# A post-layernorm block of attention and mixture of experts, fp32: V and row-sum strips grouped over two steps, and the token list made by matmuls

## The reference

```python
def _L0_attn_ref(x, wq, bq, wk, bk, wv, bv, wo, bo):
    def proj(w, b):
        return (x @ w.T + b).reshape(B, S, HEADS, HEAD_DIM).transpose(0, 2, 1, 3)
    q = proj(wq, bq)
    k = proj(wk, bk)
    v = proj(wv, bv)
    scores = jnp.einsum('bhqd,bhkd->bhqk', q, k) / scale
    probs = jax.nn.softmax(scores, axis=-1)
    ctx = jnp.einsum('bhqk,bhkd->bhqd', probs, v)
    ctx = ctx.transpose(0, 2, 1, 3).reshape(B, S, HIDDEN)
    return ctx @ wo.T + bo
...
    # _L0_ffn_ref: 8 experts of 256, each token goes to its best 2, plus a shared expert of 512
    scores = xf @ gate_w.T
    ew, ei = jax.lax.top_k(scores, TOP_K)
    ew = jax.nn.softmax(ew, axis=-1)
    routed = jnp.einsum('te,ted->td', comb, expert_out)
    shared = jax.nn.silu(xf @ sh_gate.T) * (xf @ sh_up.T) @ sh_down.T
    sgate = jax.nn.sigmoid(xf @ se_gate_w.T)
    return (routed + sgate * shared).reshape(Bb, Tt, Cc)
x = _layernorm(x + _L0_attn_ref(x, ...), axis=-1)
x = _layernorm(x + _L0_ffn_ref(x, ...), axis=-1)
```

## Time and profile before

| | |
|---|---|
| median of 3 runs | 2303.1 us (2297.88 to 2305.36) |
| the profiled execution | 2299.8 us, its span 2298.1 us |
| PE busy | 2130.9 us (93%) |
| PEld, DVE, ACT, POOL busy | 1177.7, 1212.6, 851.8, 953.1 us |
| mean granted clock of PE | 0.972 |
| DMA | 202.83 MB, mean 88 GB/s |

### The profile page before, as it was taken

How to read it: one execution, slowest core, us unless ns; L and a number is a source line. 1 busy time by engine, 2 the same in 40 slices (tenths; PEclk the granted TensorE clock), 3 DMA queues, 4 the chain that set the end, 5 groups by cost and what they waited for, 6 DMA issues and landing times. The chain is left out here.

```text
span 2298.1 us, 34596 instructions
## 1 busy us (share of the span) xinstructions
PE 2130.9 (93%) x9524; PEld 1177.7 (51%) x9525; DVE 1212.6 (53%) x2169; ACT 851.8 (37%) x1508; POOL 953.1 (41%) x926
## 2 busy tenths in 40 slices
PE   7999999999999999999999986791899999999997
PEld 5544445445445445445555422470754444445886
DVE  6767665567665566665567723450222222223875
ACT  2355553355553355554355662320111111111332
POOL 1245753454753454754454564427021111112651
PEclk9999999999999999999999998895999999999999
DMA  4230333221433221333221303560132222223762
GB/s 137 65 71 29 94 70 89 80 61 30 100 68 93 80 48 42 98 70 76 95 55 26 75 11 111 197 256 0 53 105 90 91 90 84 90 91 116 228 184 77
DMA packets 96850, 202.83 MB, mean 88 GB/s; under 512 B 26912, under 2 KB 27424, under 8 KB 94752
## 3 DMA queue, kind: packets, MB, share of 16 engines
q1 hardware_dynamic: 83744, 165.04, 24.6%
q0 software_dynamic: 12928, 35.70, 5.7%
HBM read 110.68 MB, written 39.13 MB: 65 GB/s over the span
## 5 line engine op out<-in xcount | busy, mean ns | idle before, releaser
L765 DVE TENSOR_REDUCE max_half<-ps_side 128x1 f32<-128x512 f32 x1024 | 663.5, 683 | 335.4 <-PE ps_side L532 326.1
L683 ACT ACTIVATE probs<-ps_s 128x512 f32<-128x512 f32 x1024 | 573.4, 596 | 485.9 <-PE ps_s L549 391.2
L469 POOL TENSOR_TENSOR acc<-probs 128x512 f32<-128x512 f32 x384 | 484.7, 1289 | 486.5 <-ACT probs L683 480.8
L549 PE MATMUL ps_s<-kq_stack 97*128 97x512 f32 x1024 | 461.5, 454 | 23.5 <-ACT probs L683 14.4
L532 PE MATMUL ps_side<-kq_stack 96*128 96x512 f32 x1024 | 399.8, 401 | 10.9 <-DVE max_half L765 7.2
L549 PEld LDWEIGHTS ps_s<-kq_stack 97*128 97x128 f32 x1024 | 192.6, 189 | 361.0 <-ACT probs L683 222.3
L560 PE MATMUL ps_ctx<-probs,v_sb 128*32 128x512 f32 x2048 | 274.5, 608 | 0.0
L1433 PE MATMUL ps_gu<-gu_sb,xT_e 128*128 x576 | 261.3, 596 | 0.5 <-issue 0.3
L1331 POOL DMA_INDIRECT x_g<-x,who_all x72 | 67.8, 941 | 389.0 <-PE ps_t L1423 325.7
L532 PEld LDWEIGHTS ps_side<-kq_stack 96*128 96x128 f32 x1024 | 195.9, 191 | 44.9 <-DVE max_half L765 13.8
L1433 PEld LDWEIGHTS ps_gu<-gu_sb,xT_e 128*128 128x128 f32 x576 | 103.7, 190 | 107.7 <-issue 107.3
(11 more groups left out here) (194 smaller groups left out, 2477.5 us busy)
## 6 DMA issues: line engine op xcount, KB each, us to landing
kq_stack<-kq SPq DMA_DIRECT2D x192, 256.0 KB, 5.1
y_slots<-y_t SPq DMA_DIRECT2D x72, 256.0 KB, 2.3
res<-inv_rows SPq DMA_DIRECT2D x128, 64.0 KB, 2.0
probs<-x SPq DMA_DIRECT2D x16, 512.0 KB, 5.1
x_r<-x SPq DMA_DIRECT2D x32, 256.0 KB, 3.7
x_t<-x SPq DMA_DIRECT2D x32, 256.0 KB
gu_sb<-wgu SPq DMA_DIRECT2D x8, 1024.0 KB, 14.9
out<-gu_sb SPq DMA_DIRECT2D x32, 256.0 KB, 2.6
```

Source lines behind the costliest of these rows:

```text
L469: nc.gpsimd.tensor_tensor(acc[:, h, :], probs[:, (loc - 1) % 2, h, :] if j == 1 else acc[:, h, :], probs[:, loc % 2, h, :], ALU.add).then_ ...
L549: nc.tensor.matmul(ps_s[:, (loc * HG + h) % RING, :], k_stack[par][0:3 * HD + 1, h, kt * P:(kt + 1) * P], q_stack[par][0:3 * HD + 1, h, ha ...
L683: nc.scalar.activation(probs[:, loc % 2, h, :], ps_s[:, (loc * HG + h) % RING, :], ACT.Exp, scale=HD ** -0.5).then_inc(probs_ready, 1)
L765: nc.vector.reduce_max(max_half[:, u // 2, u % 2:u % 2 + 1], bank, AX.X).then_inc(side_free, 1)
```

## The change

1. `weighted` for two steps is called at the end of the odd step, followed by `row_sums`: one group of strips per two steps. So the probabilities need three buffers (`PROBS`). The middle one lies in the place of V's low weights `wv_lo`, which are saved to DRAM at the start and loaded back before each later making of V. The exponentials wait for the strips three steps before.
2. The projection pieces are at slots 0, 4, 8, ... 60 of the group, one per step.
3. The banks of V's and the output's tiles are turned by three, and waits at the batch's edge follow the new buffers.
4. The token list: for each slot of the list a matmul sums one-hot rows (place in the tile) times one-hot columns (tile) scaled with the token number, 64 matmuls of 128 x 128 x 72 into one bank, prepared by DVE in eight parts (two behind each of tiles 3 to 6), done by PE two parts behind each of tiles 4 to 7, copied by DVE after tile 7. The scatters, the table and its load are gone.

```diff
@@ -31,13 +31,14 @@
 SLOTS = 4
-PROJ_FROM, PROJ_EVERY, PROJ_UNIT = 2, 3, 14
+PROJ_FROM, PROJ_EVERY, PROJ_UNIT = 0, 4, 16
 LOW_LATER = 2
...
 FOLD = 2
+PROBS = 3
 FOLD_DVE = 1
@@ -87,6 +88,7 @@
+    wv_lo_kept = nc.dram_tensor("wv_lo_kept", (P, C, D), F32, kind="Internal").ap()
     inv_rows = nc.dram_tensor("inv_rows", (HG, HALF), F32, kind="Internal").ap()
@@ -107,6 +109,8 @@
         wv_hi = sb("wv_hi", [P, C, D], F32R)
+        with nc.sbuf_tensor("probs_mid", [P, HG, HALF], F32) as probs_mid:
+            pass
         wv_lo = sb("wv_lo", [P, C, D], F32R)
@@ -122,7 +126,12 @@
         v_sb = sb("v_sb", [P, KT, D])
-        probs = sb("probs", [P, 2, HG, HALF])
+        probs_outer = sb("probs_outer", [P, 2, HG, HALF])
+        def probs(loc, h):
+            return probs_mid[:, h, :] if loc % PROBS == 1 else probs_outer[:, loc % PROBS // 2, h, :]
         ctx_sb = sb("ctx_sb", [P, G, S])
...
@@ -199,9 +209,13 @@
+        def tail_bank(i):
+            return ps_side[:, (i + SIDE_RING) % TAIL_RING, :]
         def res_of(t):
-            return x_nat[:, t - 2, :] if 2 <= t < 6 else res[:, t % 2, :]
+            return probs_mid[:, t - 2, :] if 2 <= t < 6 else res[:, t % 2, :]
@@ -325,6 +339,11 @@
                                              for h in (1, 2)} if x_chunks else {})
+                if not last and g == G - 1:
+                    sp.wait_ge(pv_done, (b + 1) * BSTEPS - FOLD)
+                    sp.wait_ge(sum_done, (b + 1) * SUMS - 1)
+                    sp.sem_inc(passed_sp, 1)
+                    sp.dma_start(wv_lo[:].bitcast(F32), wv_lo_kept).then_inc(wv_moved, 16)
                 if not (last and g == G - 1):
@@ -367,6 +386,8 @@
             spread(0, 0)
+            sp.wait_ge(wv_split, C)
+            sp.dma_start(wv_lo_kept, wv_lo[:].bitcast(F32)).then_inc(wv_moved, 16)
             row(-1, -1, 0, False)
@@ -466,8 +487,8 @@
                         pool.wait_ge(folded, (b * FOLDS + folds(loc) - 2) * FOLD_POOL + h + 1)
-                    nc.gpsimd.tensor_tensor(acc[:, h, :], probs[:, (loc - 1) % 2, h, :] if j == 1 else acc[:, h, :],
-                                            probs[:, loc % 2, h, :], ALU.add).then_inc(folded, 1)
+                    nc.gpsimd.tensor_tensor(acc[:, h, :], probs(loc - 1, h) if j == 1 else acc[:, h, :],
+                                            probs(loc, h), ALU.add).then_inc(folded, 1)
@@ -559,7 +580,7 @@
                                             v_sb[:, kt, (g * HG + h) * HD:(g * HG + h + 1) * HD],
-                                            probs[:, loc % 2, h, :], start=kt == 0, stop=kt == KT - 1)
+                                            probs(loc, h), start=kt == 0, stop=kt == KT - 1)
                 done.then_inc(pv_done, 1)
@@ -599,13 +620,13 @@
                         if loc == 0 and slot < SIDE_RING:
-                            pe.wait_ge(tail_free, b * TAIL + KT - (2 - slot if slot < 2 else 0) - (slot < 2))
+                            pe.wait_ge(tail_free, b * TAIL + KT - (SIDE_RING - 1 - slot))
                         for kind, u, place in side_in(last, loc, slot):
                             side_unit(b, b * G + g, g, kind, u, place)
-                        if slot == SLOTS - 1:
-                            weighted(b, loc)
-                            if loc % FOLD == FOLD - 1:
-                                row_sums(b, loc)
+                        if slot == SLOTS - 1 and loc % FOLD == FOLD - 1:
+                            for done in range(loc - FOLD + 1, loc + 1):
+                                weighted(b, done)
+                            row_sums(b, loc)
@@ -628,13 +649,14 @@
                 pe.wait_ge(side_free, base_of(b * G + G))
+                pe.wait_ge(wv_moved, 16 * (b + 2))
                 for t in range(KT):
-                    v_tile(b * TAIL + KT + t, t, ps_side[:, t % TAIL_RING, :], TAIL_RING)
+                    v_tile(b * TAIL + KT + t, t, tail_bank(t), TAIL_RING)
                 pe.wait_ge(wo_in, 16 * (b + 1))
...
                         pe.wait_ge(ctx_done, (b + 1) * G * NHALF - (t == 0))
-                    o_tile(b * TAIL + 2 * KT + t, t, ps_side[:, (KT + t) % TAIL_RING, :],
+                    o_tile(b * TAIL + 2 * KT + t, t, tail_bank(KT + t),
                            [wo[:, g, :] for g in range(G)])
...
@@ -669,18 +691,18 @@
                 act.wait_ge(scores_ready, b * HEADS_B + HG * loc + h + 1)
-                if loc >= 2:
-                    act.wait_ge(pv_done, b * BSTEPS + loc - 1)
-                    if h < FOLD_POOL:
-                        act.wait_ge(folded, (b * FOLDS + folds(loc - 2) - 1) * FOLD_POOL + h + 1)
-                    else:
-                        act.wait_ge(folded_dve, (b * FOLDS + folds(loc - 2) - 1) * FOLD_DVE + h - FOLD_POOL + 1)
-                else:
-                    if h == 0:
-                        act.wait_ge(tail_free, b * TAIL + KT // 2 * (loc + 1))
-                    if loc == 0:
-                        act.wait_ge(x2_out[h + 2], 16 * (b + 1))
-                nc.scalar.activation(probs[:, loc % 2, h, :], ps_s[:, (loc * HG + h) % RING, :],
+                if loc >= PROBS:
+                    act.wait_ge(pv_done, b * BSTEPS + loc - PROBS + 1)
+                    act.wait_ge(sum_done, b * SUMS + (loc - PROBS) // FOLD + 1)
+                elif loc == 0:
+                    act.wait_ge(tail_free, b * TAIL + (KT if isinstance(b, int) and b == 0 else h + 1))
+                elif loc == 1:
+                    if isinstance(b, int) and b == 0:
+                        act.wait_ge(wv_moved, 16)
+                    act.wait_ge(x2_out[h + 2], 16 * (b + 1))
+                elif h == 0:
+                    act.wait_ge(tail_free, b * TAIL + KT)
+                nc.scalar.activation(probs(loc, h), ps_s[:, (loc * HG + h) % RING, :],
                                      ACT.Exp, scale=HD ** -0.5).then_inc(probs_ready, 1)
...
@@ -1079,6 +1101,14 @@
+TABLE_PARTS = 8
+PART = 2 * TT // TABLE_PARTS
+COUNT_COLUMNS_AFTER = 3
+TABLE_AFTER = {3: (0, 1), 4: (2, 3), 5: (4, 5), 6: (6, 7)}
+LOOK_UP_AFTER = {4: (0, 1), 5: (2, 3), 6: (4, 5), 7: (6, 7)}
+WHO_AFTER = 7
 def combine_plan():
...
@@ -1255,17 +1289,12 @@
                 load_tile(t)
-            sp.wait_ge(made, 5)
-            sp.dma_start(table.rearrange("(p n) a -> p (n a)", p=P), zero_table[:]).then_inc(zeroed, 16)
             for e in range(E):
...
                 load_tile(t + 4)
-                if t == COVER - 3:
-                    sp.wait_ge(scattered, 16 * 2 * TT)
-                    sp.dma_start(who_all[:], table.rearrange("(p n) a -> p (n a)", p=P)).then_inc(who_in, 16)
@@ -1308,21 +1337,10 @@
             after(nc.gpsimd.memset(all_ones[:], 1.0))
-            after(nc.gpsimd.memset(zero_table[:], 0))
             after(nc.gpsimd.affine_select(out=tri[:], in_=all_ones[:], compare_op=ALU.is_gt, fill=0.0, base=0,
...
             after(nc.gpsimd.memset(minus_half[:], -0.5))
-            pool.wait_ge(placed, 1)
-            pool.wait_ge(zeroed, 16)
-            pool.sem_inc(passed, 1)
-            for t in range(TT):
-                for v in range(2):
-                    nc.gpsimd.indirect_dma_start(
-                        table, bass.IndirectOffsetOnAxis(ap=col_i[4][:, v, t:t + 1].bitcast(U32), axis=0),
-                        token[:, t:t + 1], None).then_inc(scattered, 16)
-            pool.wait_ge(who_in, 16)
+            pool.wait_ge(who_known, 1)
             pool.sem_inc(passed, 1)
@@ -1458,6 +1476,14 @@
+            def look_up(part):
+                pe.wait_ge(part_made, part + 1)
+                for c in range(PART):
+                    done = nc.tensor.matmul(ps_who, in_tile[:, part % 2, c, :], of_tile[:, part % 2, c, :],
+                                            start=part == 0 and c == 0, stop=part == TABLE_PARTS - 1 and c == PART - 1)
+                done.then_inc(part_read, 1)
             def expert_of(t):
@@ -1482,11 +1508,16 @@
                 if t == 1:
-                    pe.wait_ge(made, 6)
+                    pe.wait_ge(made, 5)
                     pe.wait_ge(visits, 1)
...
                     nc.tensor.matmul(ps_total, all_ones[:], flat, start=True, stop=True).then_inc(counted, 1)
+                if t == COUNT_COLUMNS_AFTER:
+                    pe.wait_ge(ranked, 1)
+                    nc.tensor.matmul(ps_count, all_ones[:], tri[:], start=True, stop=True).then_inc(columns_made, 1)
+                for part in LOOK_UP_AFTER.get(t, ()):
+                    look_up(part)
@@ -1725,7 +1756,8 @@
                 link(v.tensor_tensor(big[3], src[:], first[:], ALU.subtract))
-                link(v.tensor_tensor(big[3], big[3], ps_rank.rearrange("p (t e) -> p t e", e=E), ALU.add))
+                v.tensor_tensor(big[3], big[3], ps_rank.rearrange("p (t e) -> p t e", e=E), ALU.add).then_inc(ranked, 1)
+                dve.wait_ge(ranked, 1)
                 return src
@@ -1758,15 +1790,35 @@
                 link(v.tensor_copy(rows[:, 1], col_i[1][:]))
```

(27 more changed lines are left out.)

36 lines of the change are left out of this document (20 added, 16 removed).

## The result

The kernel after takes 2375.05 us (2373.86 to 2376.1 in four runs), the kernel before 2303.39 beside it: a ratio of 1.0315 [1.0297, 1.0333]. The change makes the kernel slower, close to the forecast of 2374. The profiled execution took 2376.1 us, its span 2374.4.

The account below looks back on a forecast made before the run. PE's own instruction stream bounds the kernel, with a stall in the shared expert's tiles and attention partly paced by the score ring. Terms -51 - 39 + 58 + 5 + 4 + 55 + 42 = +74 on 2299.8: 2374 us, range 2308 to 2418.

Parts of the forecast that it names:

- The list: MoE token list by matmuls: 65 us of stall removed, 14 us of PE passes added, DVE's work hidden; net -51 us.
- A pass: One of 128 fp32 lookup passes on PE: 0.11 us each, 14 us together, up to 22.
- the hole: PE idle among the shared expert's tiles during GpSimd's token-list scatters; 65.0 us go if they made it; staying: 2439, chance 0.04.
- The rule weighed against it: Skill's rule that block crossings in instruction fetch are mostly hidden; by it the 65 us have another cause and 2439 results.
- Strips in one group: Attention, merged V strips: seven pairs of steps 61.6 us against 64.45, gain 2.8 in each of 14 groups, -39 us.
- the rival in which the pairs gain nothing: Attention: even steps run into score ring and DVE's bank releases, pairs keep 9.2 us; 2413 us, chance 0.10.
- The end of the group: From T, step 14's scores: late last piece delays POOL's split and folds, next group T + 13.5, not 7.7; +58 us.
- the copies, hidden under POOL's delay: SP's head-stack copies start at T + 6.2, first head landed at T + 12.9; no added cost where POOL splits weights.
- the one group without split: Group before the last two: stack copies not hidden, next group's first maximum at T + 12.9 instead of 8.0, +5 us.
- the prologue's: Prologue: same lateness of the stack copies behind the last projection piece, once, +4 us.
- V's weights: Reload of V's low weights behind twelve copies lands at T + 26, V began about T + 7.7; 18.3 x 3, +55 us.
- The clock: PE's clock drops after new long waits: 2.7 us at 11 waits, 4 at three longer, +42; staying full: 2332, chance 0.17.

Follow-up runs that it names:

- moe_only: Kernel before with only the token list changed, made by matmuls, its attention untouched: 2246.42 us, ratio 0.9765.
- scatter_64: moe_only plus 64 scatters of the old shape whose result nobody reads: 2247.04 us, beside a kernel before of 2246.42.
- Scatter_64_b: The kernel of scatter_64 run again unchanged: 2322.78 us, ratio 1.0090, beside a kernel before of 2302.71.
- early_even: Kernel after with V's low weights reloaded ahead of the twelve copies and projection pieces in each step's first slot, the last at 52: 2244.78 us, ratio 1.0000.
- old_slots: Kernel after with the projection pieces back at their old slots, the last at 53 instead of 60: 2297.33 us, ratio 0.9996.
- early_plain: early_even with V's strips again after each step instead of merged for two steps: 2260.15 us, ratio 1.0062.
- Split_last: Kernel after with POOL's split of the next weights after the fold of step 15, not step 13: 2366.73 us, ratio 1.0292.
- wv_first: Kernel after with the reload of V's low weights issued ahead of the twelve copies into the head stacks: 2323.88 us, ratio 1.0352.

## Why the prediction was right, step by step

**The sum held at its two halves.** Attention was to gain 39 and to lose 58, 5, 4, 55 and 42, net 125 lost: measured 127.9 by the profile. The list was to gain 51: 51.6 by the profile, 53.5 by moe_only. That 2375 came so close to 2374 is in part luck: the forecast puts +74 on a kernel before of 2299.8, and measured are +71.7 on 2303.4.

**The list.** A pass was taken at 0.11 us and measures 0.109, which makes 14.0 for 128 (forecast 14). Two parts were to take DVE 5.8 and take 5.9, hidden. The 65 us of the hole are gone, as "if they made the hole" had it. Here the prediction rested on a condition that it did not know: that the hole comes at all. In two of the sets the kernel before takes 2246 instead of 2300, and there the new MoE part gains nothing: scatter_64, which holds it, takes 2247.04 against 2246.42. For such an occasion I estimate the whole change at 2375 against 2246, a ratio of 1.057; it wasn't run there.

Why the kernel before, without its hole, isn't faster than the new list by the 14 of the lookups isn't shown, since no profile of it was taken on such an occasion. Rows of the others make a cause likely: its list is then late by about as much. The first scatter starts 40.7 us after the first transpose of the MoE's x, the last at 120.5 (1532.22 and 1612.03, less 1491.53), and scatter_64 shows that the pace is the same without a hole. Then come its landing (2.1, scatter_64's median), the load of the table up to the first gather (3.5, from 1664.67 to 1668.13), and from the gather to the first expert tile on PE 3.8 (1671.91). That is an estimate of 129.9 for the start of the expert tiles. In moe_only they start at 130.3 (1618.92 less 1488.65), with the 14 of lookups before them. So what the scatters spare PE it would lose in waiting for the list.

**The rule weighed against it.** The gap is PE's instructions coming singly while small scatters are issued: 7 matmuls in 20 us instead of 113. The Trainium skill (Runtime: NRT & Kernel Launch, Instruction fetch mechanics) says that the next block of a program is fetched during the current one and that a crossing is mostly hidden. Scatter_64 agrees with that. Scatter_64_b disagrees only if its gaps are fetches, as the prediction thought, at one packet of that queue in 90 us and 76 us lost. That is read from gaps that nothing else ends and from that queue; it isn't shown. One instruction in 1.4 us isn't what a single late block would look like, so each instruction may be held up by itself. Why it happens on some occasions only was not found.

**Strips in one group: the term that was too large.** Seven pairs were walked as 61.6 us, 8.80 each with all that comes on top, and 2.8 saved per group. Here the six pairs after the first take 53.54. The first is slowed by the clock; early_even has the same pieces in it and takes 8.59 at full clock (851.55 to 860.14). Together 62.1, so 2.3 per group and 32 in all, not 39. What failed is not only the hand walk's size but its name: old_slots has merged strips too and 71.55 per group, early_plain has plain strips and 73.36 at the new kind of slots. The gain belongs to merged strips and evenly spread pieces together. For merging alone at the old slots (0.6) the rival in which the pairs gain nothing was nearer than the forecast; at the even slots (2.1) it wasn't.

**The end of the group.** Split T + 4.5 (4.54 measured), folds T + 8.7 (8.69), PE's wait 4.6 (4.44), next group T + 13.5 (14.32). The missing 0.8 is the row sums themselves, 1.9 instead of 0.97 at half the clock. The waits are thirteen, as forecast, of 4.38 to 5.41; the fourteenth in the row is 1.41 at attention's last step, where the kernel before waits 1.43 too. Old_slots shows both new waits gone with the piece at slot 53. Split_last shows what the prediction said of the copies, hidden under POOL's delay: take the cover away and 44 us more of waiting for them appear in its place.

**Copies.** T + 6.2 (6.65 measured). The wait in the one group without split, forecast at 5, is 3.01 in the trace, and the prologue's, forecast at 4, is 3.65:

```profile
90.01 0.79 PE L553 MATMUL ps_side<-kq_stack 96*128 96x512 f32 x1 [3.65 <-DMA kq_stack<-kq]
```

**V's weights: the term that was too small.** Forecast T + 26, measured T + 29.4 to 29.8: the copies start 1.5 later than assumed, and the 1 MB takes 7.05 from issue to use (410.86 to 417.91), not 5.8. PE's own wait is 15.2 to 15.6, forecast about 11. V starts at T + 7.2 in the kernel before, so it is late by 22.5 three times, 67 us, not 55.

**The clock: right for the groups, too large behind V.** In and after a 4.4 us wait the granted clock is at 1.2 GHz for 6.8 us, as in the earlier trace rows. It was to cost 2.7, for which the prediction shows no working. The pair that follows takes 10.20 instead of the 8.59 of early_even, so 1.6, and another 0.9 is in the row sums: 2.5. For the three longer waits it took 4 each. From V's start to the end of the next batch's first pair the kernel after takes only 0.2, 0.5 and 1.5 longer than the kernel before, so the clock costs about 2 there and not 12. Why so little wasn't tested.

**What cancelled.** In the group shown, the pairs are 0.5 us longer than forecast, the end 0.8 longer, and the clock behind it 1.1 less: 72.15 became 78.06, by 5.9, where the terms give 5.7. Over the nine intervals inside the first three batches, leaving out the very first, the growth is 4.3 to 6.0, mean 5.2. Over a batch's end it is 20.4, 21.0 and 22.3, where the forecast's terms (-2.8, 18.3 and 4 for the clock) give 19.5: V's start is 4.2 later than forecast each time, and the clock takes back about 3. With the measured sizes the terms of attention are -32, 58, 3, 4, 67 and 30 (eleven times 2.5, and 2), net 130, where the forecast had 125. The strips (7) and V (12) were off one way and the clock (12) the other. The sum was nearer than its terms were.

## What to carry to other kernels

When work is spread out evenly to smooth one engine, look at what hangs on its last piece: here moving it by seven slots of 64 put POOL's fold, twelve copies and a 1 MB load late. Old_slots and the kernel after differ in the slots alone. The late piece makes the pairs shorter by 26 us (62.1 for 63.96, fourteen times) and attention longer by 77 (1619.4 for 1542.5), so its late end costs about 103, four times what the smoother middle gives. The reload of V's weights behind the copies costs PE 42 us of waiting with the early piece too (old_slots); issued ahead of them it costs no wait (wv_first). Undoing the first wait in such a place shows the second one; move the piece, or the transfers behind it, rather than swap the order on one queue. And a gain that consists of removing a stall is only as large as the stall is on the occasion on which it is measured: run the kernel before beside it each time.

The version to keep is early_even, with the list by matmuls: 2244.78 us, no faster than the kernel before where that takes 2246, but 130 us under the kernel after (in another set; the profiles' attention and MoE parts differ by 133 and 2), and free of the scatters that cost the kernel before 56 on other occasions. Moe_only, with attention untouched, does as much at 2246.42.

## What was not expected of the hardware

The same program on the same chip had a median of 2247.04 us in one set (all runs 2242.67 to 2250.76) and of 2322.78 in another (2318.18 to 2325.11), with PE's clock at 1.0 in one and at 0.67 to 0.5 in the other while POOL issued scatters of 128 numbers of 4 bytes. Eight profiles of kernels without scatters, four in either kind of set, have MoE parts within 3.1 us of each other (753.5 to 756.6). The hole isn't a fixed property of the program.
